# Graph-and-convolution GRU block: messages and similarity coordinates from one fp32 matmul in the GRU stage, distance operands turned by TensorE, four batches' distances in one burst

## What is computed

```python
h = relu(_bn(_conv1d(xc, conv1_w, 0)))           # 1 tap
h = _bn(_conv1d(h, conv2_w, 8))                  # 17 taps
x_conv = relu(h + xc)
s = x @ w_se.T + b_se                            # 3 coordinates a node
dist = sq[:, :, None] + sq[:, None, :] - 2.0 * einsum('bnd,bmd->bnm', s, s)   # sq = sum(s*s)
A = exp(-dist) * mask
msg = relu(x @ w_msg.T + b_msg)
x_nmp = einsum('bnm,bmd->bnd', A, msg)
gi = concat([x_conv, x_nmp]) @ w_ih.T + b_ih     # three gates
gh = x @ w_hh.T + b_hh                           # three gates
r, z = sigmoid(gi_r + gh_r), sigmoid(gi_z + gh_z)
out = layernorm(x + (1 - z) * tanh(gi_n + r * gh_n) + z * x)
```

## Time and profile before

| | us |
|---|---|
| runs of the kernel before | 335.26, 336.97, 337.74 |
| median | 336.97 |
| profiled execution: span, first to last instruction | 335.7 |
| profiled execution: its own device time | not listed apart from the three runs |
| busy: PE, DVE, ACT, POOL | 314.9, 267.9, 177.6, 23.9 |

### The profile page before, as it was taken

The page is one execution under the profiler, slowest core; times in us unless marked ns, Lnnn a source line. Parts: engine busy times, 40 slices in busy tenths (PEclk is TensorE's granted clock), DMA queues, the critical chain, the costliest instruction groups (busy, mean ns, idle before and its releaser), DMA issues.

```text
span 335.7 us, 4839 instructions
## 1 busy us (share of the span) xinstructions
PE 314.9 (94%) x1474; PEld 253.9 (76%) x1474; DVE 267.9 (80%) x646; ACT 177.6 (53%) x352; POOL 23.9 (7%) x51
## 2 busy tenths in 40 slices
PE   1879999999999999999999999999999999999970
PEld 1657788878887888888887888888888888788850
DVE  4799879749979969749979979858979978864686
ACT  4777455347666333547767424537767444434450
POOL 3100000000000140000000050000000041000122
PEclk9997999999999999999999999999999999999996
DMA  6600710362010131372000122281100103140002
GB/s 173 242 0 3 250 63 2 125 208 75 33 52 11 62 124 37 87 269 82 31 31 31 62 77 79 69 278 69 52 31 31 62 8 140 39 126 0 2 31 94
DMA packets 12268, 27.24 MB, mean 81 GB/s; under 512 B 1371, under 2 KB 1760, under 8 KB 12128
## 3 DMA queue, kind: packets, MB, share of 16 engines
q1 hardware_dynamic: 12256, 27.09, 24.3%
HBM read 22.89 MB, written 4.19 MB: 81 GB/s over the span
## 4 chain that ended last, share of the span: by engine, by line
PE 87%; DVE 5%; DMA 3%; ACT 1%; SPq 1%; issue 0%; POOL 0%; POOLq 0%; ACTq 0%; DVEq 0%
PE bank L287 86%; DMA r<-xt_dram 2%; PE bank L439 2%; DMA xs<-xt_dram 1%; DVE x L784 1%; ACT H L486 0%; DVE x_lo L813 0%; ACT x_hi L480 0%; DVE cw_lo L796 0%; DVE EF L836 0%; POOLq L75 0%; POOL rstd L686 0%; SPq L212 0%; DVE xn L964 0%; DVE hn L877 0%
## 5 line engine op out<-in xcount | busy, mean ns | idle before, releaser
L287 PE MATMUL bank<-V_hi,cw_hi 128*128 128x512 f32 x160 | 70.9, 443 | 0.7 <-DVE cw_lo L796 0.6
L287 PE MATMUL bank<-V_lo,cw_hi 128*128 128x512 f32 x160 | 65.0, 406 | 0.0
L287 PE MATMUL bank<-V_hi,cw_lo 128*128 128x512 f32 x160 | 64.8, 405 | 0.0
L287 PE MATMUL bank<-x_hi,w_hl 128*128 128x512 f32 x128 | 47.4, 425 | 2.2 <-DVE x_lo L813 2.2
L287 PEld LDWEIGHTS bank<-V_hi,cw_hi 128*128 128x128 f32 x160 | 30.6, 191 | 8.7 <-issue 0.7
L287 PEld LDWEIGHTS bank<-V_hi,cw_lo 128*128 128x128 f32 x160 | 30.6, 191 | 8.4
L287 PEld LDWEIGHTS bank<-V_lo,cw_hi 128*128 128x128 f32 x160 | 30.5, 191 | 7.2
L287 PE MATMUL bank<-r,msg 128*128 128x256 f32 x128 | 35.8, 402 | 0.0
L510 ACT ACTIVATE msg<-bank 128x256 f32<-128x256 f32 x32 | 12.2, 382 | 44.2 <-PE bank L287 44.1
L287 PE MATMUL bank<-c_hi,w_hl 128*128 128x512 f32 x96 | 34.7, 395 | 0.0
L287 PE MATMUL bank<-m_hi,w_hl 128*128 128x512 f32 x96 | 34.6, 395 | 0.0
(11 more groups left out here) (128 smaller groups left out, 654.6 us busy)
## 6 DMA issues: line engine op xcount, KB each, us to landing
adj<-adj_dram SPq DMA_DIRECT2D x16, 512.0 KB, 3.7
x<-xt_dram SPq DMA_DIRECT2D x16, 256.0 KB, 3.1
xn<-xn_dram SPq DMA_DIRECT2D x16, 256.0 KB, 4.5
out_dram<-xn SPq DMA_DIRECT2D x16, 256.0 KB, 2.3
xs<-xt_dram SPq DMA_DIRECT2D x14, 256.0 KB, 4.0
xn<-wcv_dram SPq DMA_DIRECT2D x1, 1024.0 KB, 6.7
r<-xt_dram SPq DMA_DIRECT2D x2, 256.0 KB, 5.4
adj<-wsm_dram SPq DMA_DIRECT2D x1, 512.0 KB, 9.4
```

The source lines that it names most:

```text
L287: return nc.tensor.matmul(out, lhs, rhs, start=start, stop=stop, skip_group_check=True)
```

## The change

- `u_rows`, `affine`, `square_rows`, the old `operands`, `message_half` and `message_sum` go. `messages` moves from the mix stage to the GRU stage, two batches behind each `conv1`. It is now one fp32r matmul of the bias with 128 rows of contraction (rows 2 to 127 are zero) and 264 columns, and two true fp32 matmuls of 132 columns (128 message features, 3 coordinates, 1 empty) with raw x (`xs`) as the stationary operand. ScalarE's `message` takes relu of one part to `msg` and copies the coordinates to `S`.
- `rows` on VectorE builds, nodes on partitions, 16 columns a batch for left and right operands (11 small instructions, three of its own waits). `turn_rows` on TensorE transposes them (four transposes for four batches), ScalarE's new `operands` copies them to `LR`.
- `distances` does four batches at once, 8 matmuls over four 32-partition groups into four banks.
- `rows(g+1, 0)` and `turn_rows(g+1, 0)` stand in chunk 2 of the GRU stage, `rows(g, 1)` at the start of VectorE's mix stage, `turn_rows(g, 1)` behind `conv2(g, 0)`. The mix stage on TensorE begins with `conv2(g, 0)`.
- conv1 has one bank in place of two. The reload of `xs` waits for the messages of the chunk that lay there. A has four buffers in z and r. The small inputs bse and selb go, wm (128 x 132) comes.

```diff
             def conv1(g, k):
                 pe.wait_ge(x_ready, 4 * g + k + 1)
-                if k >= 2:
-                    pe.wait_ge(h_ready, 4 * g + k - 1)
+                if k >= 1:
+                    pe.wait_ge(h_ready, 4 * g + k)
...
+            def messages(g, b, first=False):
+                if b >= 2:
+                    pe.wait_ge(msg_ready, 8 * g + b - 1)
+                out, k = both_blocks(msg_bank[b % 2]), b // 2
+                src = x_first[:, k - 2] if first and k >= 2 else xs[:, k % 2]
+                rows = bmsg_r[:, :].rearrange("p (o d) -> p o d", o=1).broadcast_to([P, MB, MW])
+                mm(out, ones_r[:, :], rows, start=True)
                 for mb in range(MB):
+                    at = (b % 2) * N + mb * P
+                    last = mm(out[:, mb], src[:, at:at + P], wm[:, :], stop=(mb == MB - 1))
+                last.then_inc(msg_done, 1)
+
+            def turn_rows(g, q):
+                pe.wait_ge(rows_ready, 2 * g + q + 1)
+                for i in range(2):
+                    for mb in range(MB):
+                        last = nc.tensor.transpose(lr_bank[q][:, i * N + mb * P:i * N + (mb + 1) * P],
+                                                   f32(U[:, i, mb]).rearrange("p b k -> p (b k)"), cst[:, IDN:IDN + P])
+                last.then_inc(lr_done, 1)
+
+            def distances(g, q):
                 pe.wait_ge(lr_ready, 2 * g + q + 1)
+                if q == 1:
+                    pe.wait_ge(exp_ready, 8 * g + 4)
                 for mb in range(MB):
+                    for i in range(4):
+                        rows = slice(32 * i, 32 * i + KIND)
+                        last = mm(dist_bank[i][:, mb * N:(mb + 1) * N], LR[rows, 0, mb * P:(mb + 1) * P],
+                                  LR[rows, 1, :], start=True, stop=True)
...
             def mix_stage(g, first):
-                u_rows(g, 0)
-                messages(g, 0)
...
-                u_rows(g, 1)
-                if not first:
-                    turn(g - 1, NC - 1)
                 for n in range(NP):
                     conv2(g, n, first)
-                    if 1 <= n < GB:
-                        messages(g, n)
-                    if n < GB:
-                        distances(g, n)
+                    if n == 0:
+                        if not first:
+                            turn(g - 1, NC - 1, False)
...
+                        distances(g, 0)
+                        pe.wait_ge(msg_ready, 8 * g + 7)
+                        turn_rows(g, 1)
+                    if n == 3:
+                        distances(g, 1)
                     if n >= 1:
-                        gather(g, n - 1)
+                        gather(g, n - 1, first)
...
                 part(z_bank, HHZ, xk, start=True).then_inc(gx_done, 1)
+                if k == 2 and not last:
+                    pe.wait_ge(y_ready, 4 * g + 1)
+                    turn_rows(g + 1, 0)
...
             def gru_stage(g, last):
...
                     if not last:
                         conv1(g + 1, k)
+                        messages(g + 1, 2 * k)
+                        messages(g + 1, 2 * k + 1)
...
+            def message(g, b):
+                act.wait_ge(msg_done, 8 * g + b + 1)
+                out = both_blocks(msg_bank[b % 2])
+                nc.scalar.activation(msg[:, b], out[:, :, 0:P], ACT.Relu)
+                nc.scalar.activation(S[:, b // 4, :, b % 4, :], out[:, :, P:MW], ACT.Copy).then_inc(msg_ready, 1)
...
             def gru_stage(g, last):
                 for k in range(NC):
                     if not last:
                         split_x(g + 1, k, False)
+                        if k == 2:
+                            operands(g + 1, 0)
...
                     if not last:
+                        message(g + 1, 2 * k)
                         early_hi(g + 1, k)
+                        message(g + 1, 2 * k + 1)
...
+            def rows(g, q, first=False):
+                dve.wait_ge(msg_ready, 8 * g + 4 * q + 4)
+                if not first or q == 1:
+                    dve.wait_ge(lr_done, 2 * g + q)
...
+                nc.vector.tensor_copy(hi, s2)
+                TT(sq3[:, :, :], s, s, ALU.mult).then_inc(rows_step, 1)
+                dve.wait_ge(rows_step, at + 1)
+                TT(lo, s2, f32(hi), ALU.subtract)
+                TS(twice[:, :, :, 0, :], f32(hi), 2.0, None, ALU.mult)
+                TT(sq[:, :, :], sq3[:, :, 0:1], sq3[:, :, 1:2], ALU.add).then_inc(rows_step, 1)
+                dve.wait_ge(rows_step, at + 2)
+                TS(twice[:, :, :, 1, :], f32(lo), 2.0, None, ALU.mult)
+                for dst in (sqn[:, :, :], left[:, :, SQH:SQH + 1], right[:, :, SQH + 2:SQH + 3]):
+                    last = STT(dst, sq[:, :, :], -1.0, sq3[:, :, 2:3], ALU.mult, ALU.subtract)
...
             def gru_stage(g, last):
                 for k in range(NC):
                     rk, zk, hk = r[:, k % 2, :], z[:, k % 2, :], hn[:, k % 2, :]
                     if not last and k == 0:
                         split_x(g + 1, 0, False)
+                    if not last and k == 2:
+                        rows(g + 1, 0)
```

More of the change, by code:

```diff
@@ L295, in conv1 @@
                 pe.wait_ge(x_ready, 4 * g + k + 1)
-                if k >= 2:
-                    pe.wait_ge(h_ready, 4 * g + k - 1)
-                three(conv1_bank[k % 2][:, :], w_hi[:, W1, :], w_lo[:, W1, :], chunk(x_hi, k), chunk(x_lo, k),
+                if k >= 1:
+                    pe.wait_ge(h_ready, 4 * g + k)
+                three(conv1_bank[:, :], w_hi[:, W1, :], w_lo[:, W1, :], chunk(x_hi, k), chunk(x_lo, k),
                       True, True).then_inc(conv1_done, 1)
[L301 to L309, removed]
@@ L364, in conv2 @@
                     pe.wait_ge(cw_ready, n + 1 if n < 6 else n)
[L365 to L366 removed]
+                if n == 0:
+                    if first:
+                        pe.wait_ge(lr_ready, 1)
+                    else:
+                        pe.wait_ge(y_ready, 4 * g - 1)
+                if n == 1:
+                    pe.wait_ge(msg_ready, 8 * g + 8)
                 if n >= 2:
@@ L549, in shared @@
                 src, dst = conv2_bank[(3 * j) % 2][:, :], (S_first if first else S_later)[j]
-                if not first and j == 0:
-                    src = src.rearrange("p (h n) -> p h n", h=2)
                 nc.scalar.activation(dst, src, ACT.Identity,
@@ new lines, in mix_stage @@
+            def mix_stage(g, first):
+                if first:
+                    slot_high(E1, E_all[:, 1], 1)
+                    shared(g, 0, first)
+                    weights(g, 0)
+                    sum_hi(0)
+                    weights(g, 1)
+                    sum_hi(3)
+                    operands(g, 1)
+                    weights(g, 2)
+                    gates_hi()
+                    slot_high(F0, F_one, 2)
+                    weights(g, 3)
+                    taps_hi()
+                    slot_high(F1, F_one, 3)
+                else:
+                    late_hi(g, 2)
+                    late_hi(g, 3)
+                    shared(g, 0, first)
+                    weights(g, 0)
+                    weights(g, 1)
+                    operands(g, 1)
+                    weights(g, 2)
+                    weights(g, 3)
+                sums_hi(g, 0)
+                shared(g, 1, first)
+                weights(g, 4)
+                if first:
+                    slot_high(E3, E_all[:, 3], 3)
+                    slot_high(F2, F_one, 4)
+                sums_hi(g, 1)
+                weights(g, 5)
+                if first:
+                    slot_high(F3, F_one, 5)
+                relu2(g, 0)
+                weights(g, 6)
+                shared(g, 2, first)
+                relu2(g, 1)
+                weights(g, 7)
+                sums_hi(g, 2)
+                relu2(g, 2)
+                sums_hi(g, 3)
@@ L912, in product @@
                 src, shr = conv2_bank[n % 2][:, :], (S_first if first else S_later)[j]
-                if not first and j == 0:
-                    src, dst = (t.rearrange("p (h n) -> p h n", h=2) for t in (src, P1[:, side, :]))
-                else:
-                    src, shr = grid(src), grid(shr)
-                STT(dst, src, v(NSC2 if side else SC2), shr, ALU.mult, ALU.add).then_inc(prod_used, 1)
+                STT(dst, grid(src), v(NSC2 if side else SC2), grid(shr), ALU.mult, ALU.add).then_inc(prod_used, 1)
             def conv_sum(g, c, first):
@@ L979, in late_differences @@
                     late_differences_f(g, k)
-                norm(square_rows, g, 0)
-                norm(message_sum, g, 0)
-                norm(residual, prev, NC - 1)
+                rows(g, 1, first)
                 if first:
```

398 lines of the change are left out of this document (152 added, 246 removed).

## The result

The changed kernel takes 347.84 us (median of 6 runs, 345.59 to 348.70) against 337.26 us (6 runs): ratio 1.0305, interval 1.0266 to 1.0344. The forecast was 348. The profiled execution has a span of 344.0 us and took 346.49 us, the second shortest of the six. Its differences from the trace of before add up to 8.3 us, where the medians differ by 10.6.

The account below looks back on a forecast made before the run. PE's summed work bounds the kernel. A period adds -4.5 + 3.8 + 2.4 + 3.0 = +4.7 us, three periods +14, the first group -3: 336.97 + 14 - 3 = 348 us, range 338 to 356 (the forecast's own 342 to 354).

Parts of the forecast that it names:

- PE's own work: PE over one period: removed 11.4 us, added messages 4.5, transposes 0.9, bursts 1.5; sum -4.5 us (-5.8 to +0.6).
- wait A: Chunk 2 of the GRU stage: PE waits at turn_rows(g+1, 0) for DVE's rows(g+1, 0), 3.8 us a period.
- wait B: Start of the mix stage: PE waits at conv2(g, 0) for early_lo(g, 3), 2.4 us a period (2.0 to 3.2).
- clock: Behind wait A and wait B: one stretch at 1.2 GHz each, 3.0 us a period (from below zero, above 6.0).
- first group: Setup and first mix stage: shorter PE work against a later conv2(0, 1), -3 us in all (-8 to +1).
- The message batch: PE's new messages: bias matmul 0.12 plus four records of 0.11, 0.56 us a batch (0.47 to 0.96).
- The burst: Eight distance matmuls on PE, 0.75 us a burst, two a period; 0.43 if four partition groups ran fully beside each other.
- The 1.03 us a batch that went: Between products of the mix stage: messages and distances leaving PE save 1.03 us a batch, seven times, 7.2 us.
- That the clock holds: Rival: the slow stretch belonged to the setup's repeated gaps, not a single wait; 339 us, chance 0.22.
- That the first group decides: Rival: in the setup, messages fill PE's gaps and keep its clock up, price -8; 332 us, chance 0.10.
- That both waits grow: Rival: rows at 2.6, a second slow stretch behind A, message record near 0.16; 360 us, chance 0.13.
- That the waits are not there: Rival: DVE or PE runs another order than the one read; about 320 us, within the 0.10 for faster.

Follow-up runs that it names:

- experiment 1: Changed kernel with turn_rows(g+1, 0) and its copy to LR moved from chunk 2 to chunk 3 of the GRU stage: 330.56 us, ratio 0.9815 to the kernel before.
- experiment 8: The kernel of experiment 6 with the messages' bias matmul on 2 rows of contraction in place of 128: 336.44 us, ratio 0.9992 to the kernel before.
- experiment 2: Kernel before the change plus one PE wait in chunk 2 of the GRU stage, for early_lo(g+1, 1) (V_lo): 352.20 us, ratio 1.0438.
- Experiment 4: Changed kernel with early_hi and early_lo of chunk 3 ahead of its tanh chain on ACT and DVE: 342.95 us, ratio 1.0167 to the kernel before.
- experiment 6: Experiment 5 plus conv1(g+1, 3) ahead of turn(g, 2) on PE and the residual behind the differences on DVE: 325.90 us, ratio 0.9690 to the kernel before.
- experiment 10: Kernel before the change plus one PE wait in chunk 2 of the GRU stage, for DVE's x_lo of that chunk: 349.60 us, ratio 1.0363.
- 5: Changed kernel with the edits of experiments 1 and 4 together: 326.44 us, ratio 0.9698 to the kernel before.
- 7: Experiment 6 plus four setup banks for conv1 and relu1(0, k+1) ahead of early_hi(0, k) and messages on ACT: 326.79 us, ratio 0.9711 to the kernel before.
- 9: Experiment 6 with the 8 distance matmuls of a burst ordered batch by batch, not group by group: 326.72 us, ratio 0.9664 to the kernel before.
- 3: Kernel before the change plus one PE wait in chunk 2 of the GRU stage, for ACT's x_hi of that chunk: 341.02 us, ratio 1.0117.

## Why the prediction was right, step by step

| term of a period | forecast | measured | from |
|---|---|---|---|
| PE's own work | -4.5 | -5.0 | 74.80 - 77.14 - 2.7 (B) in experiment 1 |
| wait A | 3.8 | 3.7 | 166.36 - 162.68 |
| wait B | 2.4 | 2.7 | 185.81 - 183.13 |
| clock | 3.0 | 2.8 | what is left: 81.30 - 77.14 + 5.0 - 3.7 - 2.7 |
| sum | +4.7 | +4.2 | 81.30 - 77.14 |
| first group | -3 | -4.8 | 61.32 - 66.09 |

The measured terms of a period are those of the second, in the profiled executions.

*PE's work.* The message batch came out at 0.57 (0.56 forecast): true fp32 with 132 columns costs by its columns, and no weight load sticks out. The burst was mis-sized: 0.75 against 0.61 with its entry, and the eight matmuls alone took 0.44, my lower bound, the one in which the four groups run fully beside each other. By its parts the sum is -11.4 + 4.6 + 0.8 + 1.2 = -4.8. The 1.03 us a batch that went held changes between row tiles, and the 128-row bias matmul is what keeps them out of the new messages: with 2 rows, the whole gain of the reordered kernel is gone (experiment 8). I gave that edit no step of its own; the 0.12 that I took for it was right, but I had not seen that on 2 rows it would have cost 0.5 (0.12 + 0.39).

*A.* Right in place, cause and size, shown by taking it away (1) and by putting it alone into the kernel before (2). `rows` took 1.4 us (1.7 forecast), and ACT's two messages moved relu1's followers by little.

*B.* Right in place and cause. A part of it is an order that nothing demands: V behind the tanh chain on ACT and DVE. Experiment 4 took 0.9 us of it away. That the rest is the chain from conv1(3) is read from the timelines; only experiment 6, where that chain starts earlier, bears on it (1.1 in place of 1.5 us).

*The clock.* One stretch for each wait, 3.0 us, against 2.8 measured: near, but partly by luck. The starts confirm the 2.8: ten matmuls behind the second B took 3.99 us, behind the first, at 2.4 GHz, 2.50, so that stretch cost 1.5, and the one behind the second A some 1.4. The forecast gave A and B the same price. Behind A it came every time, and behind the first A it was longer, some 2.4 us of loss. Behind B it came twice of three, and without A never, so the price of B alone is lower. The longer stretch happened to make up for the one that stayed out. Without the clock term the forecast would have been 339, below every run of the changed kernel.

*The total.* 348 against 347.84 is nearer than the terms deserve. In the profiled executions three periods came to +13.1 (forecast +14) and the first group to -4.8 (forecast -3), together 8.3 where the forecast had 11. The medians differ by 10.6; the first group's gain of only 3.0 to 3.8 in the other traces is a part of that difference, the rest stays open.

*The rivals.* That the clock holds: out, by windows at 0.54 and by experiment 2. That the first group decides: it gained 4.8, not 8, since the first product began 3 us later. That both waits grow: B by 0.3 us, A not at all. That the waits are not there: out.

*Where the expected gain went.* It is real: with A gone and B at 1.1 us the same design is 3% faster than before (experiment 6), 22 us faster than as it was changed. The change saved 5 us of PE's time in a period and put two instructions where their operands could not yet be ready.

## What to carry to other kernels

On the engine that sets the end, a new instruction is placed by asking when its last operand can be ready at the earliest, followed back through every engine's order to an event on the same engine; if that event is the instruction just ahead, the whole chain is a wait, however short its links, and one chunk later it is free. A wait of a few us also costs clock: here a slow stretch was mostly worth 1.4 to 1.6 us, once 2.4, and came behind every wait of 3.3 us or more. And when a TensorE stretch is full of small matmuls, look for changes between row tiles before counting columns: padding the contraction with zeros to 128 rows can be the larger gain (10.5 us in experiment 8, where the change as a whole had saved 5 us of PE's time in each of three periods).

## What the runs showed of the hardware that I had not expected

A 2-row bias matmul among 128-row ones costs 0.39 us more than the same with 126 rows of zeros. Eight 16-row matmuls of 256 columns on four partition groups take 0.44 us, as long as two on one group, and in either order of the groups: matmuls on different groups start within hundredths of a us of each other even where another of the same group stands between them in the program. And waits of PE in the GRU and mix stages that the view puts at 3.3 to 3.5 us were followed by 1.2 GHz each time (9 of 9: the changed kernel, experiments 2 and 4), those of 2.4 to 2.7 us sometimes (2 of 3 in the changed kernel, 2 of 3 in experiment 10, none of 3 in experiment 1), those of 1.5 us (experiments 4 and 5), 1.1 us (6, 7 and 9) or 0.7 us (3) never, while the earlier trace rows has a case with 1.21 us in the setup, in a stretch with other gaps. How long the clock stays low varies too: behind the first A of the changed kernel it was low from 85.60 to 90.50, behind the others for less.
